# Mixture of experts by scattered rows: from every expert over every token to 23 tiles of 256 chosen rows

## The reference

```python
score = jax.nn.relu(xf @ rw1 + rb1) @ rw2 + rb2          # router, 512 hidden, 8 scores
_, topi = jax.lax.top_k(score, TOP_K)                     # TOP_K = 2 of 8
gate = jax.nn.softmax(jnp.where(mask, score, -jnp.inf), axis=-1)
for e in range(N_EXPERTS):                                # 8 experts
    h = jax.nn.relu(xf @ W1[e] + b1[e])                   # 128 -> 512
    y = h @ W2[e] + b2[e]                                 # 512 -> 128
    out = out + gate[:, e:e + 1] * y
x = x + gb * out
```

## Time and profile before

| | |
|---|---|
| median of 3 runs | 1224.33 us (1223.57 to 1225.33) |
| the profiled execution, its own time | 1223.92 us |
| its span, first to last instruction | 1222.1 us |
| mean granted TensorE clock | 0.974 |
| PE busy | 1129.2 us, 92% |
| DVE busy | 829.3 us, 68% |
| ACT busy | 813.3 us, 67% |
| POOL busy | 28.9 us, 2% |

### The profile page before, as it was taken

The page is one execution under the profiler, slowest core; times in us unless marked ns, Lnnn a source line. Parts: engine busy times, 40 slices in busy tenths (PEclk is TensorE's granted clock), DMA queues, the critical chain, the costliest instruction groups (busy, mean ns, idle before and its releaser), DMA issues.

```text
span 1222.1 us, 21866 instructions
## 1 busy us (share of the span) xinstructions
PE 1129.2 (92%) x9020; PEld 634.8 (52%) x9020; DVE 829.3 (68%) x1172; ACT 813.3 (67%) x1495; POOL 28.9 (2%) x73
## 2 busy tenths in 40 slices
PE   4865999888999999999999999999999699999998
PEld 3534788732533333333333333333333379798887
DVE  3857333369999999999999999999930622222222
ACT  2646443344089999989999999999898554444342
POOL 0002000000000000000000000000000000000000
PEclk9996999979989999999999999999999899999999
DMA  9000000000000000000000000000000000000000
GB/s 383 21 1 0 1 1 1 1 0 1 1 2 2 2 2 2 1 2 2 2 2 2 2 2 2 2 2 2 2 2 2 1 1 1 10 1 9 6 3 9
DMA packets 5432, 14.84 MB, mean 12 GB/s; under 512 B 352, under 2 KB 4576, under 8 KB 4832
## 3 DMA queue, kind: packets, MB, share of 16 engines
q1 hardware_dynamic: 5056, 10.84, 2.3%
q10 hardware_dynamic: 288, 2.76, 0.5%
HBM read 12.29 MB, written 1.05 MB: 11 GB/s over the span
## 4 chain that ended last, share of the span: by engine, by line
DVE 48%; PE 46%; ACT 4%; issue 1%; DMA 1%; SPq 0%; DVEq 0%; ACTq 0%
DVE mx L1269 41%; PE ps L990 9%; PE ps L721 6%; PE ps L722 6%; PE ps L723 6%; PE ps L870 4%; PE ps L842 4%; PE ps L758 1%; PE ps L811 1%; PE ps L971 1%; PE ps L787 1%; DMA x<-x_in 1%; PE ps L851 1%; DVE Qs L1257 1%; DVE z L1042 1%
## 5 line engine op out<-in xcount | busy, mean ns | idle before, releaser
L1269 DVE TENSOR_REDUCE mx<-ps 128x2 f32<-128x1024 f32 x512 | 587.7, 1213 | 14.8 <-PE ps L811 14.1
L534 ACT ACTIVATE probs<-ps 128x512 f32<-128x512 f32 x1024 | 540.7, 598 | 57.3 <-PE ps L870 48.3
L870 PE MATMUL ps<-Qb,Ks 32*128 32x512 f32 x1024 | 328.7, 496 | 0.5 <-ACT probs L534 0.5
L842 PE MATMUL ps<-probs,V 128*16 128x256 f32 x4096 | 320.6, 386 | 7.1 <-ACT U L528 7.1
L811 PE MATMUL ps<-Ks,Qb 32*128 32x512 f32 x1024 | 257.3, 499 | 8.2 <-DVE mx L1269 5.2
L870 PEld LDWEIGHTS ps<-Qb,Ks 32*128 32x128 f32 x1024 | 150.5, 182 | 214.7 <-issue 124.7
L581 ACT ACTIVATE eh<-ps,MW 128x512 f32<-128x512 f32 x128 | 87.5, 688 | 83.4 <-PE ps L723 82.9
L842 PEld LDWEIGHTS ps<-probs,V 128*16 128x16 f32 x4096 | 67.2, 94 | 134.1 <-issue 76.5
L990 PEld LDWEIGHTS ps<-MW,eh 128*128 128x128 f32 x1024 | 118.3, 192 | 2.4
L811 PEld LDWEIGHTS ps<-Ks,Qb 32*128 32x128 f32 x1024 | 95.3, 182 | 46.1 <-DVE mx L1269 32.0
L990 PE MATMUL ps<-MW,eh 128*128 128x128 f32 x1024 | 119.2, 275 | 0.0
(11 more groups left out here) (218 smaller groups left out, 1085.9 us busy)
## 6 DMA issues: line engine op xcount, KB each, us to landing
MW<-moe_in SPq DMA_DIRECT2D x1, 4454.0 KB, 23.9
FW<-ffn_in SPq DMA_DIRECT2D x1, 2824.5 KB, 12.5
SW<-spectral_in ACTq DMA_DIRECT2D x1, 1479.5 KB, 9.9
DW<-mods_in ACTq DMA_DIRECT2D x1, 1219.0 KB, 6.4
x<-x_in SPq DMA_DIRECT2D x4, 256.0 KB, 10.9
out<-x SPq DMA_DIRECT2D x4, 256.0 KB, 2.3
AW<-attn_in SPq DMA_DIRECT2D x1, 836.5 KB, 13.8
Qb<-mT SPq DMA_DIRECT2D x32, 8.0 KB
```

Of the source, the lines that this page charges most:

```text
L534: act.activation(probs[:, 4 * (s % 4) + g, :], score(n), ACT.Exp, scale=SCALE1) \
L842: last = pe.matmul(ps[32 * g:32 * g + VW, 6, queries], V[:, kt, col:col + VW], probs[:, 4 * (s % 4) + g, queries], start=(kt == 0 and half ...
L870: pe.matmul(score(n), Ks[rows, hg, kt * P:kt * P + P], Qb[rows, hg, :], start=True, stop=True).then_inc(sem.st_ready, 1)
L1269: dve.tensor_reduce(mx[:, k // 16 % 2, k % 16 // 4, k % 4, 2 * pair:2 * pair + 2], ps[:, at:at + 2, :], AX, ALU.max).then_inc(sem.bank_rea ...
```

## The change

The router runs for all four blocks first. DVE then gives each pair of token and choice a slot: expert times 2048 plus its rank among the rows of that expert, the rank by matmuls with a triangle of ones (`places`). POOL copies each row of 128 features, its row number and its gate (`zx`, 132 floats) to that slot of `buf` in HBM, 128 rows by one indirect DMA, 32 in all. `buf` has been filled with zeros during the attention, by 11 DMAs on SP. DVE works out how many tiles of 256 slots each expert has, and from that a table of 23 tiles (16 full ones and at most 7 partial ones): which expert, which place.

Then 23 times: SP loads the tile's expert number and place from SBUF into registers, and issues four DMAs: the rows `gz`, the first weights, the bias and the second weights of that expert. PE turns the rows, ACT modulates them (`modulate`), DVE splits weights and rows (`weights`, `second_rows`), PE does `up` with 256 moving columns and `down` with 8 fp32 products, DVE scales by gate and `gb`, and POOL writes the 2 times 128 result rows to `yk` in HBM by token and choice, by two indirect DMAs. Empty slots carry a row number out of bounds, so they are not written. At the end SP reads `yk` back in four blocks, DVE adds the two choices to `x`, SP stores.

```diff
+SLOTS = 256
+TILES = TOK * 2 // SLOTS + EXP - 1
+ROW = 132
...
-            sp.dma_start(MW[:, :], moe_in).then_inc(sem.moe_in, 16)
+            sp.dma_start(MW[:, 0:w1_at], moe_in[:, 0:w1_at]).then_inc(sem.moe_in, 16)
+            sp.dma_start(MW[:, w1_at:w1_at + P], moe_in[:, b2_at:b2_at + P]).then_inc(sem.moe_in, 16)
...
+                if 2 <= grp < 13:
+                    sp.dma_start(buf_rows[:, 12 * ROW * (grp - 2):12 * ROW * (grp - 1)], zeros[:, :]).then_inc(sem.buf_zero, 16)
...
+            sp.wait_ge(sem.sent, 16 * 2 * NT)
+            for i in range(TILES):
+                e = sp.value_load(expert[0:1, i:i + 1], min_val=0, max_val=EXP - 1)
+                r = sp.value_load(place[0:1, i:i + 1], min_val=0, max_val=8 * EXP)
+                if i > 3:
+                    sp.wait_ge(sem.scaled, 2 * (i - 3))
+                sp.dma_start(gz[:, i % 4, :, :], pairs[bass.ds(r * P, P), :, :]).then_inc(read_in[i % 4], 16)
+                if i > 2:
+                    sp.wait_ge(sem.w1_lo, i - 2)
+                    sp.wait_ge(sem.eh_copied, 4 * (i - 2))
+                sp.dma_start(w1[:, i % 3, :], moe_in[:, bass.ds(e * FF + w1_at, FF)]).then_inc(up_in[i % 3], 16)
+                sp.dma_start(b1[:, i % 3, :], moe_in[:, bass.ds(e * FB + b1_at, FB)]).then_inc(up_in[i % 3], 16)
+                if i > 2:
+                    sp.wait_ge(sem.ey_ready, i - 2)
+                sp.dma_start(w2[:, i % 3, :], moe_in[:, bass.ds(e * FF + w2_at, FF)]).then_inc(w2_in[i % 3], 16)
...
+                for t in range(4 * b, 4 * b + 4):
+                    for c in range(2):
+                        pool.indirect_dma_start(buf[:, :], bass.IndirectOffsetOnAxis(slot[:, t, c:c + 1], 0), zx[:, t, c, :], None,
+                                                bounds_check=EXP * TOK - 1, oob_is_err=False).then_inc(sem.sent, 16)
+            for i in range(TILES):
+                pool.wait_ge(sem.target_ready, i + 1)
+                for q in range(2):
+                    pool.wait_ge(sem.scaled, 2 * i + q + 1)
+                    pool.indirect_dma_start(yk[:, :], bass.IndirectOffsetOnAxis(target[:, i % 2, q:q + 1], 0), ye[:, i % 2, q, :], None,
+                                            bounds_check=2 * TOK - 1, oob_is_err=False).then_inc(added[i % 2], 16)
...
-                for e in range(2 * b, 2 * b + 2):
-                    split_experts(e)
...
+            def modulate(i):
+                act.wait_ge(sem.gT_ready, i + 1)
...
+                act.activation(gh[:, i % 2, :], ps[:, 6 + i % 2, 0:SLOTS], ACT.Identity, bias=modv[:, 9:10], scale=cv[:, 3:4]) \
+                   .then_inc(sem.gh_ready, 1)
...
+                act.activation(ghh[:, i % 2, :], ps[:, 6 + i % 2, 0:SLOTS], ACT.Identity, bias=modv[:, 9:10], scale=cv[:, 3:4]) \
+                   .then_inc(sem.hh_ready, 1)
...
+            pe.wait_ge(sem.rh_copied, 4 * TB)
+            for _ in range(30):
+                pe.matmul(bank(1), hT1[0][:, 0:P], hT1[0][:, 0:512], start=True, stop=True)
...
+            for i in range(TILES):
+                if i + 1 < TILES:
+                    up(i + 1)
+                if i + 2 < TILES:
+                    turn_rows(i + 2)
+                down(i)
...
+            for i in range(TILES):
+                if i + 2 < TILES:
+                    weights(i + 2)
+                    second_rows(i + 2)
+                if i > 1:
+                    dve.wait_ge(added[i % 2], 32 * (i // 2))
+                dve.tensor_scalar(target[:, i % 2, :], gz[:, i % 4, :, P], float(2 * TOK), None, ALU.add).then_inc(sem.target_ready, 1)
+                dve.wait_ge(sem.ey_ready, i + 1)
+                for q in range(2):
+                    dve.scalar_tensor_tensor(out=ye[:, i % 2, q, :], in0=ps[:, 2 + i % 2, q * P:q * P + P],
+                                             scalar=gz[:, i % 4, q, P + 1:P + 2], in1=gb[:, 1, :],
+                                             op0=ALU.mult, op1=ALU.mult).then_inc(sem.scaled, 1)
```

More of the change, by code:

```diff
@@ L15 @@
 BF16 = mybir.dt.bfloat16
+I32 = mybir.dt.int32
 ALU = mybir.AluOpType
@@ L109, in adaln_pair @@
         fcbg = sb("fcbg", [P, 1])
+        zeros = sb("zeros", [P, 12 * ROW])
+        index = sb("index", [P, 201], I32)
+        index_f = sb("index_f", [P, 201])
+        lower = sb("lower", [P, P])
+        buf = nc.dram_tensor("buf", (P * ROW, ROW), F32).ap()
+        yk = nc.dram_tensor("yk", (2 * TOK, P), F32).ap()
         l0 = ExitStack()
@@ new lines, in adaln_pair @@
+            slot = sb("slot", [P, NT, 2], I32, where=l2)
+            tiles_of = sb("tiles_of", [P, EXP], where=l2)
+            over = sb("over", [P, EXP, 8], where=l2)
+            tri = sb("tri", [P, EXP, EXP], where=l2)
+            starts = sb("starts", [P, EXP], where=l2)
+            ends = sb("ends", [P, EXP], where=l2)
+            past = sb("past", [P, TILES, EXP], where=l2)
+            past_tiles = sb("past_tiles", [P, TILES, EXP], where=l2)
+            expert_f = sb("expert_f", [P, TILES], where=l2)
@@ new lines, in hidden @@
+            def hidden(i):
+                act.wait_ge(up_in[i % 3], 32 * (i // 3 + 1))
+                if i > 1:
+                    act.wait_ge(sem.ey_ready, i - 1)
+                for fb in range(FB):
+                    act.wait_ge(sem.eh_ready, 4 * i + fb + 1)
+                    act.activation(eh[:, i % 2, fb, :], up_bank(fb)[:, 0:SLOTS], ACT.Relu, bias=b1[:, i % 3, fb:fb + 1]) \
+                       .then_inc(sem.eh_copied, 1)
+            modulate(0)
+            modulate(1)
+            hidden(0)
@@ new lines, in places @@
+            def places(tb):
+                pe.wait_ge(sem.picked, tb + 1)
+                if tb > 1:
+                    pe.wait_ge(sem.placed, tb - 1)
+                to = ps[:, 2 + tb % 2, 0:4 * EXP].rearrange("p (q e) -> p q e", e=EXP)
+                pe.matmul(to, cw["ones"][0:1, :], wide(index_f[0:1, base_at:base_at + EXP], [1, 4, EXP], 1),
+                          start=True, stop=False, skip_group_check=True)
+                pe.matmul(to, lower[:, :], picks[:, 4 * tb:4 * tb + 4, :], start=False, stop=False, skip_group_check=True)
+                for q in range(3):
+                    pe.matmul(to[:, q + 1:4, :], cw["ones"], wide(picks[:, 4 * tb + q, :], [P, 3 - q, EXP], 1),
+                              start=False, stop=False, skip_group_check=True)
+                pe.matmul(to, cw["ones"], wide(run[:, tb, :], [P, 4, EXP], 1), start=False, stop=True,
+                          skip_group_check=True).then_inc(sem.place_ready, 1)
@@ L1011, in moe @@
                                      start=True, stop=True)
                 last.then_inc(sem.b2_ready, 1)
-                down(1)
-                for e in range(3, EXP):
-                    up(e)
-                    down(e - 1)
-                down(EXP - 1)
-            moe(0)
-            with pe.Fori(1, TB) as tb:
-                moe(tb)
+            router(0)
+            router(1)
+            router_scores(0)
+            router(2)
+            router_scores(1)
+            pe.wait_ge(sem.lower_made, 1)
@@ new lines, in _ @@
+            pe.wait_ge(sem.index_real, 1)
+            places(0)
+            router(3)
+            router_scores(2)
+            places(1)
+            router_scores(3)
+            places(2)
+            places(3)
+            pe.matmul(ps[:, 0, 0:EXP], cw["ones"], run[:, TB, :], start=True, stop=True).then_inc(sem.count_ready, 1)
+            pe.wait_ge(sem.eb2_scaled, 1)
+            for tb in range(TB):
+                bias_sums(tb)
+            pe.wait_ge(sem.rh_copied, 4 * TB)
+            for _ in range(30):
+                pe.matmul(bank(1), hT1[0][:, 0:P], hT1[0][:, 0:512], start=True, stop=True)
@@ new lines, in down @@
+            def down(i):
+                pe.wait_ge(w2_in[i % 3], 16 * (i // 3 + 1))
+                pe.wait_ge(sem.eh_copied, 4 * i + 4)
+                if i > 1:
+                    pe.wait_ge(sem.scaled, 2 * (i - 1))
+                for q in range(2):
+                    for fb in range(FB):
+                        last = pe.matmul(ps[:, 2 + i % 2, q * P:q * P + P], eh[:, i % 2, fb, q * P:q * P + P],
+                                         w2[:, i % 3, fb * P:fb * P + P], start=(fb == 0), stop=(fb == FB - 1))
+                last.then_inc(sem.ey_ready, 1)
@@ new lines, in _ @@
+            dve.wait_ge(sem.pick_step, 1)
+            for tb in range(TB):
+                pick(tb)
+                gates(tb)
+                slots(tb)
+            dve.wait_ge(sem.count_ready, 1)
+            dve.tensor_tensor(over[:, :, :], wide(ps[:, 0, 0:EXP], [P, EXP, 8], 2),
+                              wide(index_f[:, limit_at:limit_at + 8], [P, EXP, 8], 1), ALU.is_gt).then_inc(sem.tab_step, 1)
+            dve.wait_ge(sem.tab_step, 1)
+            dve.tensor_reduce(tiles_of[:, :], over[:, :, :], AX, ALU.add).then_inc(sem.tab_step, 1)
@@ new lines, in _ @@
+            dve.wait_ge(sem.tab_step, 2)
```

(6 more changed lines are left out.)

403 lines of the change are left out of this document (261 added, 142 removed).

## The result

The changed kernel takes 1178.48 us (median of 4 runs, 1174.47 to 1180.68), the kernel before 1223.95 beside it (1223.53 to 1225.33). The ratio is 0.962, with a 95% interval of 0.959 to 0.965: 45.5 us less, where 62 were forecast. The changed kernel scatters more than the one before: 6 us between its slowest and fastest run, against 2.

The account below looks back on a forecast made before the run. TensorE alone was taken to set the end of the expert stage. Dispatch landed at 1037.8, first tile 1050.6, 22 more tiles to 1143.0, collection to 1160.2, plus 1.8 outside: 1162 us, 62 less; range 1137 to 1212.

Parts of the forecast that it names:

- Start, router, ranking: Before the dispatch: router starts at 973.9, first scores at 984.9, slots ready 9, 17, 24 and 30 us later.
- The scatter's price: Dispatch: each of POOL's 32 indirect DMAs costs 1.3 us, middle of bounds 0.37 and 2.3; 41.6 us in all.
- Rival 1: Tile loop: POOL binds if a scatter costs over 2.05 us; at 2.3 the time is 1207 us; chance 0.12.
- rival 2: Tile loop: SP binds; register loads at 2.3 us give 6.6 us per tile, 1215 us; chance 0.12.
- Rival 3: PE's `up`: 256 columns cost what 512 do, `up` stays 2.83 us, time 1187 us; chance 0.05.
- Rival 4: Dispatch and tiles: scatters make no progress while DVE operates; 1256 us at 1.9 per scatter; chance 0.13.
- `tab`, bias sums and PE's 30 filler matmuls fall under what follows.: Between ranking and first tile: this work is covered by the dispatch and adds nothing to the sum.
- the first tile's own chain: From the first `gz` issued near 1039, through landing, DVE's splitting, `up` and `down`, to the first result at 1050.6.
- The loop: Twenty-two more tiles at 4.2 us each, 92.4 us, ending at 1143.0; bounds 3.5 and 6.6 per tile.
- the ring of SP's weights: Tile loop: SP issues tile i+1 only after `down(i-3)`; two periods must be 7.7 us, one 3.85.
- The 0.35 that I had added for a hole: Tile loop: the stage's largest issue hole, added to 3.85 to give 4.2 us per tile.
- The end: Collection after the last tile: scalings, last scatters, reading 2.1 MB back, adds and close, from 1143.0 to 1160.2.

Follow-up runs that it names:

- the last two kernels: Changed kernel with late bias sums, four weight buffers, only tile 0's weights early; without fillers 1160.34 us, with 18 fillers 1159.75 us.

## Why the prediction was right in kind and 16 us short

**Start, router, ranking: right.** Router at 972.8 (973.9 forecast), first scores with DVE at 984.02 (984.9), first slots at 994.0 (993.9). Block 1 to 3 were later than forecast: 1007.5, 1014.8 and 1023.5 instead of 1002, 1009 and 1015. The PE clock fell to its lower level at about 1000, where the scores of a block take 6.97 us instead of 3.63, and two of PE's updates came 2.3 us late. PE's own pace weighs more: with plain writes and every update prompt, blocks 1 to 3 still follow block 0 by 11.7, 21.3 and 28.1 us (13.5, 20.8 and 29.5 here, 8, 15 and 21 forecast). It cost 2.7 us once, when POOL waited for block 1's slots ahead of its ninth scatter.

**The scatter's price: right, 1.28 us for 1.3 assumed.** The first rows of POOL:

```profile
995.13 1.28 POOL L467 DMA_INDIRECT buf<-zx,slot  x1 [24.29 <-issue]
996.72 0.97 POOL L467 DMA_INDIRECT buf<-zx,slot  x1 [0.30 <-issue]
```

The middle of a wide range happened to be the value; the argument for it (no row is near) was no better than that. A plain write of POOL costs 0.54. The landing was quicker than the 2.3 us that I had: the last scatter ends at 1038.75, and SP passes its wait for all 32 (L368) at 1040.1, 1.3 us later. The register loads were slower at this place: from there to the first `gz`, at 1042.53, SP takes 2.4 us for two of them, where I had 1.0.

```profile
L368 SPq EVENT_SEMAPHORE  x1: 17/17/17, 1040.1 to 1040.1; - x1
```

**Rivals.** Rival 1 (POOL binds the tiles) and rival 2 (SP binds) are refuted by the same trace: two scatters are 2.6 of 3.88 us, and SP's waits are mostly for PE. Behind the first tile, a register load and what goes with it cost SP 0.58 us, as the distance of its transfers in the version without fillers shows:

```profile
1049.94 0.33 SPq L381 DMA_DIRECT2D b<-moe_in  x1
1050.46 0.33 SPq L384 DMA_DIRECT2D w<-moe_in  x1
1051.57 0.33 SPq L373 DMA_DIRECT2D gz<-buf  x1
1052.67 0.33 SPq L380 DMA_DIRECT2D w<-moe_in  x1
```

0.52 between two transfers without a load, 1.10 with one. The first pair, at 2.4 us, was dearer, but it comes once. With the floor of about 600 ns of the Trainium skill ("DMA: Bandwidth & Descriptors", "Latency and other measured facts") the 0.58 agrees. Rival 3 (256 columns no cheaper) is refuted, `up` takes 1.42 us as forecast. Rival 4, the one on the slower side, is refuted: scatters stand 1.28 us apart when DVE works (1020 to 1030) and when it is idle (1031 to 1038) alike. In the tile loop, where DVE makes the copy and the subtraction that the rival named, 39 of the 46 scatters take 0.97 us, whether DVE works beside them or not. Six others are 0.03 to 0.12 us longer and the first one 0.35 (the first of the dispatch was 0.31 longer too). Had scatters stood still while DVE worked, many would have been longer by up to 1 us. The lock between DVE and POOL that the Trainium skill describes ("SBUF — State Buffer", "SBUF: two separate sides") shows nowhere in the scatters of the dispatch. What the scatters did disturb were PE's updates and SP's register-addressed transfers, which no rival named.

**The step that failed: "`tab`, bias sums and PE's 30 filler matmuls fall under what follows."** The first tile's result came at 1069.4 and not at 1050.6, 18.8 us. Of these, 3.5 are the rows, asked for at 1042.5 instead of 1039: the first scatter 1.2 us later, the hole of 2.7, the loads 1.4 more, against 1.0 less for the landing and 0.7 less for the other scatters (3.6 with rounding). The other 15.3 are nearly all the work costed at nothing. With the bias sums behind the tiles, it takes 13.5 us from the asking for the rows to the first result; here it takes 26.9, so 13.4 belong to the bias sums and fillers. The remaining 1.9 are the first tile's own chain, for which I had 11.6: in PE's order `up(0)` stands behind the turn of tile 1's rows, which SP asks for 3.7 us after tile 0's. The step hides two errors. First, I named no length for this work and no slack of its cover. PE has to make 16 transposes, 32 product instructions and 30 matmuls of 512 columns in order ahead of `turn_rows(0)`, in turn with ACT, and mostly at half clock: 23.4 us where every update is prompt (the kernel with POOL's plain writes). It begins at 1021.1, and the rows asked for at 1042.5 would be there at 1044.7, by the 2.1 us from issue to PE's start in the kernel with late bias sums. So the cover was 23.6 us, with nothing to spare. (As `up(0)` also waits for tile 1's rows, some 3.7 us more, the work would still have just fitted; that is an estimate from these two kernels.) Second, and this is what cost the time, the scatters themselves held up what they were to cover: the handshake with ACT stood still for 14 us and more, and the same work took 41.3 us, from 1021.1 to 1062.4, instead of 23.4. Taking the two out one by one showed it: fillers -6.3 us, bias sums moved -11.1 us.

**The loop: mechanism right, size off.** 4.2 us per tile forecast, 3.88 measured (85.3 us for 22 instead of 92.4), 7.1 us in favour. The 3.5 for PE and the ring of SP's weights at 3.85 were right: DVE waits for weights in 19 of the 23 tiles, 22.0 us in all, and a fourth buffer brings the period to 3.64. The 0.35 that I had added for a hole was one too many in this execution; in the second profile of the same kernel the period was 4.10. The median of the runs lies between these two executions.

**The end: right.** 17.2 us from the last result forecast, 18.0 measured. The sum in trace terms: 1160.2 + 18.8 - 7.1 + 0.8 = 1172.7. The miss would have been larger without the loop's error, which went the other way.

## What to carry to other kernels

Work that is "hidden" needs a length and a cover in the sum like any other, and the cover must be checked for what it does to the handshakes inside the hidden work: a chain that goes from engine to engine and back needs every signal on time. Filler matmuls placed ahead of a wait by program order run after the wait's condition too: if anything in front of them is late, they are on the path. And where runs of one kernel differ by 10 us, look for a ring of buffers without slack before calling it noise. A fourth buffer went with a spread of 1.3 us instead of 5.7 in one pair of kernels here, but the last two kernels, with four buffers, spread by 4.3 and 3.0 over five runs each, so that it narrows the spread is not shown.

## What the runs showed of the hardware

- While POOL builds indirect transfers, waiters see PE's semaphore updates late: mostly 0.4 to 2.4 us for those of the ranking, 2.8 to 6.5 for the token count, 7.6 to 14 for the first gate transposes; 0.2 to 1.1 us in the loop with two scatters a tile. Plain transfers to consecutive rows, built by POOL (0.54 us each) or by SP, leave them at 0.02 us or less; dropping the bounds changes nothing. Updates between ACT and DVE stay prompt. Why, no run here shows. What was told apart is the form of the transfer, not its mechanism.
- In the same stretches SP issues a transfer with an address from a register every 3.5 to 4.2 us instead of 0.52 to 0.55, one with a constant address every 0.4 to 1.4 (single run).
- One hole of 2.5 us in PE's work was followed by matmuls at the lower clock (0.41 us instead of 0.28), and 18 fillers that ended 2.9 us ahead of the first tile left it at the lower clock too.
